# A selective scan (Mamba-style) with its stage rebuilt: differences on row tiles, sums in 64x64 quarters, rows of C by DMA

## The reference, cut to what matters

```python
delta = softplus(pp[..., :D]); Bm = pp[..., D:D+N]; Cm = pp[..., D+N:]
A = -exp(A_log);  dA = delta * A;  A_bar = exp(dA)
U = X_main * (A_bar - 1)/dA * delta * Bm
H_t = A_bar_t * H_(t-1) + U_t          # per sequence, d, n, over t
y_t = sum_n C_t[n] * H_t[:, n]
Y_proj = (y * silu(Xn @ W_up2.T)) @ W_down.T + b_down
out = X_res + Y_proj
```

## Time and profile before

| | us |
|---|---|
| median of 3 runs | 694.96 |
| span of the profiled execution | 668.4 |
| first scan to last (L509) | 106.3 to 373.6 |
| TensorE busy, of the span | 546.2 (82%) |
| VectorE busy | 510.2 (76%) |
| GpSimd busy | 432.6 (65%) |
| ScalarE busy | 338.0 (51%) |

### The profile page before, as it was taken

The page is one execution under the profiler, slowest core; times in us unless marked ns, Lnnn a source line. Parts: engine busy times, 40 slices in busy tenths (PEclk is TensorE's granted clock), DMA queues, the critical chain, the costliest instruction groups (busy, mean ns, idle before and its releaser), DMA issues.

```text
span 668.4 us, 12960 instructions
## 1 busy us (share of the span) xinstructions
PE 546.2 (82%) x3471; PEld 410.1 (61%) x3472; DVE 510.2 (76%) x1227; ACT 338.0 (51%) x809; POOL 432.6 (65%) x539
## 2 busy tenths in 40 slices
PE   3598996889899989989949889980667999999990
PEld 2433344656676757666728757770535779999990
DVE  7657677999999999998999862464686776666654
ACT  1655767836576756675723144420584554444430
POOL 3205592889999999999994677756027743455550
PEclk9999997879999999999998999995687989999996
DMA  7999000020000000000120155557931121222106
GB/s 244 171 280 288 19 6 0 1 64 1 1 1 0 0 0 0 0 0 0 48 79 17 35 162 164 166 170 220 384 116 50 50 65 41 60 56 59 50 24 188
DMA packets 55017, 54.83 MB, mean 82 GB/s; under 512 B 7743, under 2 KB 44182, under 8 KB 53952
## 3 DMA queue, kind: packets, MB, share of 16 engines
q1 hardware_dynamic: 49584, 42.57, 21.2%
q0 software_dynamic: 5392, 11.76, 6.8%
HBM read 34.24 MB, written 21.12 MB: 83 GB/s over the span
## 4 chain that ended last, share of the span: by engine, by line
PE 48%; DVE 25%; issue 8%; POOL 6%; ACT 6%; DMA 5%; DVEq 1%; SPq 0%; ACTq 0%; POOLq 0%
DVE arena L509 8%; PE bank L1419 7%; PE bank L1055 6%; PE bank L1406 6%; PE bank L1057 5%; PE bank L1014 4%; POOL expert_rows L1931 4%; POOL bd L1863 2%; PE bank L1098 2%; DVE arena L470 2%; PE bank L982 2%; PE bank L1023 2%; DMA xnw<-expert_rows 2%; DMA expert_rows<-gate,zbuf 1%; PE bank L1042 1%
## 5 line engine op out<-in xcount | busy, mean ns | idle before, releaser
L509 DVE TENSOR_TENSOR_SCAN arena<-bank,arena 128x256 f32<-128x256 f32 x256 | 160.9, 667 | 8.2 <-issue 6.1
L1553 ACT ACTIVATE arena<-delta,nega 128x256 f32<-128x256 f32 (+1 forms) x256 | 108.0, 499 | 8.8 <-DVE delta L428 6.9
L1879 POOL TENSOR_TENSOR arena<-arena 128x256 f32<-128x256 f32 x116 | 89.0, 771 | 24.7 <-DVE arena L470 20.2
L1055 PE MATMUL bank<-bd,xnw 128*128 128x258 f32 x256 | 86.4, 420 | 20.3 <-DVE arena L509 16.3
L1981 POOL DMA_INDIRECT pair_rows<-w1b,xnT x48 | 50.8, 1058 | 58.2 <-DVE w1b L771 49.3
L470 DVE SCALAR_TENSOR_TENSOR arena<-arena,inva,bank 128x256 f32<-128x256 f32 x192 | 82.6, 456 | 0.1
L1854 POOL TENSOR_TENSOR bd<-cfs,btok 128x258 f32<-128x258 f32 x128 | 79.3, 640 | 0.0
L1057 PE MATMUL bank<-bd,xnw 128*128 128x256 f32 x256 | 79.3, 392 | 0.0
L1055 PEld LDWEIGHTS bank<-bd,xnw 128*128 128x128 f32 x256 | 44.7, 196 | 44.9 <-DVE arena L509 24.5
L1014 PE MATMUL bank<-arena,ident 128*128 128x256 f32 x232 | 71.0, 388 | 1.3 <-DVEq L483 0.9
L1536 ACT ACTIVATE hbuf<-bank,inva 128x256 f32<-128x256 f32 x64 | 26.8, 469 | 83.2 <-PE bank L1042 83.0
(11 more groups left out here) (294 smaller groups left out, 1099.7 us busy)
## 6 DMA issues: line engine op xcount, KB each, us to landing
expert_rows<-bd SPq DMA_DIRECT2D x8, 1024.0 KB, 9.8
xnT<-expert_rows SPq DMA_DIRECT2D x4, 1024.0 KB, 6.2
bd<-in_w SPq DMA_DIRECT2D x4, 1024.0 KB, 13.2
arena<-in_w SPq DMA_DIRECT2D x4, 1024.0 KB, 14.4
slots_in<-bd POOLq DMA_DIRECT2D x1, 3120.0 KB, 24.7
xnT<-slots_in SPq DMA_DIRECT2D x48, 65.0 KB, 1.8
xnw<-expert_rows SPq DMA_DIRECT2D x3, 1024.0 KB, 6.4
bd<-in_w SPq DMA_DIRECT2D x8, 256.0 KB, 4.2
```

Source lines behind the costliest of these rows:

```text
L509: m = V.tensor_tensor_scan(zb[:, s % 8, r, :], dw_bank(par, s)[:, r * L:(r + 1) * L], abar[:, s % 8, r, :], 0.0, ALU.add, ALU.mult)
L1055: pe.matmul(o[:, :, 0:P + 1], xT[:, par, 0, h * P:(h + 1) * P], bd[:, par, 0, 2 * n2:2 * n2 + 2, :], start=True, stop=False, skip_group_ch ...
L1553: m = nc.scalar.activation(abar[:, s % 8, r, :], delta[:, h, bass.ds(b * L, L)], ACT.Exp, scale=negs[:, h, n:n + 1])
L1879: nc.gpsimd.tensor_tensor(zb[:, s % 8, 0, :], zb[:, s % 8, 0, :], zb[:, s % 8, 1, :], ALU.add).then_inc(S["q_ready"], 1)
```

## The change

Only the scan stage and its edges change.

- Steps: step s now holds half `s // 2 % 2` of the channels and states `first_n(s)`, `first_n(s) + 1`; four steps share four states. The results live in a ring of 16 steps (before: 8 for A_bar and 8 for results), and the scan writes over A_bar in place.
- Differences (`fill`): x and B are laid out in windows of 44 time steps that give 43 differences, three windows for each half of time. The two halves of time lie on partitions 0 to 43 and 64 to 107, so that the matmuls of a pair are on different row tiles. One fill makes 4 states of one half of the channels, that is two steps, into two banks; there are two such pairs of banks. The band matrices are compact: one GpSimd operation of 516 elements for 4 states (`band`), its pattern loaded once.
- C: `c_spread` writes the 16 rows of C to DRAM and reads them back spread over all partitions, in two DMAs of 1 MB for each batch, double buffered. The split of C, the selector products and the scaled rows are gone.
- Products: one operation of 512 elements for both states of a step, result times C, on GpSimd for 14 of the 16 steps and on VectorE for steps 7 and 15 (in batch 7 for six steps).
- Sums (`y_pair`, `y_quarters`): TensorE multiplies by diagonal 64x64 matrices of 1/A (`dg`, made once by GpSimd), each 128x128 product cut into four quarters; the correction enters as the first term with weights -1 (`y_begin`), from one product on VectorE (`correction`) that reads PSUM.
- `finish` is one product with the gate out of PSUM. The output projection takes y as weights and gives tokens on partitions, so its result is added to the residual at once (`residual`, 256 elements a batch); the bias is added once on GpSimd. The 16 transposes and four sums behind the last batch are gone.
- Order: TensorE's queue is written anew, with fills of the next batch at the end of this one. ScalarE copies x instead of GpSimd. `down` of batch b comes in batch b+1.

The core of the diff (loads, names, memory layout and the other engines' deletions are cut; blank lines are left out):

```diff
+WN, WIN, WK = 3, 43, 44
+STARTS = (0, 43, 85)
+GW = WN * WIN * 4
+XW = STARTS[2] + P + 64
+BY_DVE = (7, 15)
+BY_DVE_LAST = (2, 4, 7, 10, 12, 15)
...
+        ring = arena[:, :].rearrange("p (s r l) -> p s r l", s=16, r=2)
...
+        xT = xnf[:, 0:1536].rearrange("p (a q d) -> p a q d", a=2, q=WN)
+        yg = xnf[:, 1536:2048].rearrange("p (j l) -> p j l", j=2)
+        t1 = hb[:, 0:512].rearrange("p (h l) -> p h l", h=NH2)
+        bands = [xnTw[:, :], hb[:, 2032:2032 + 4 * GW]]
...
+        def half(s):
+            return s // 2 % 2
+        def first_n(s):
+            return s // 4 * 4 + s % 2 * 2
...
+        def dw_view(s):
+            o = 2 if half(s) == 0 else 0
+            return banks[:, o:o + 2, :].rearrange("p j c -> p (j c)").rearrange("p (t n) -> p n t", n=4)
+        def c_view(par, s):
+            return cbc[par][:, first_n(s) * L:first_n(s) * L + 2 * L].rearrange("p (r l) -> p r l", r=2)
...
+            def mult(b, par, s, last=False):
+                if s == min(own_steps(last)) or s == min(k for k in own_steps(last) if k > 7):
+                    dve.wait_ge(S[f"c_in{par}{s // 8}"], c_count(b, par))
+                dve.wait_ge(S["scanned"], b * 16 + s + 1)
+                V.tensor_tensor(ring[:, s, :, :], ring[:, s, :, :], c_view(par, s), ALU.mult).then_inc(S["z_dve"], 1)
+            def correction(b):
+                dve.wait_ge(S["m_ready"], b + 1)
+                V.tensor_tensor(t1[:, :, :], xm[:, :, bass.ds(b * L, L)], bank[7][:, :].rearrange("p (h l) -> p h l", h=NH2), ALU.mult
+                                ).then_inc(S["t1_ready"], 1)
+            def finish(b):
+                dve.wait_ge(S["y_done"], b * 8 + 16)
+                dve.wait_ge(S["dn_ready"], b + 1)
+                V.tensor_tensor(yg[:, :, :], banks[:, 4:6, 0:L], gate[:, :, bass.ds(b * L, L)], ALU.mult).then_inc(S["yg_ready"], 1)
+            def residual(b, o):
+                dve.wait_ge(S["dn_ready"], b + 2)
+                if not later(b, 1):
+                    dve.wait_ge(S["bias_in"], 1)
+                t = acc[:, bass.ds(b * 2, 2), :].rearrange("p t d -> p (t d)")
+                V.tensor_tensor(t, t, o[:, 0:L], ALU.add).then_inc(S["dn_evac"], 1)
...
-                    dve.wait_ge(S["dw_ready"], b * 16 + s + 1)
-                    dve.wait_ge(S["p_free"], b * 16 + s + 1)
+                    if s % 2 == 0:
+                        dve.wait_ge(S["dw_ready"], b * 8 + s // 2 + 1)
                     for r in range(2):
-                        m = V.tensor_tensor_scan(zb[:, s % 8, r, :], dw_bank(par, s)[:, r * L:(r + 1) * L], abar[:, s % 8, r, :],
+                        m = V.tensor_tensor_scan(ring[:, s, r, :], dw_view(s)[:, 2 * (s % 2) + r, :], ring[:, s, r, :],
                                                  0.0, ALU.add, ALU.mult)
-                    m.then_inc(S["ab_free"], 1)
-                    if s >= 1:
-                        mult(b, s - 1)
-                    elif later(b, 1):
-                        mult(b - 1, 15)
+                    m.then_inc(S["scanned"], 1)
+                    if s == 0 and later(b, 1):
+                        mult(b - 1, 1 - par, 15)
+                    if s - 1 in own_steps(last):
+                        mult(b, par, s - 1, last)
                     if not later(b, 1) and s < 12:
                         dve.wait_ge(S["dve_link"], link.n)
                         if s < 4:
                             add_log(2 + s)
                         elif s >= 8:
                             last_steps(s - 8)
-                        dve_at["steps"] = link.n
+                        dve_at["steps" if s > 3 else "logs"] = link.n
+                    if s == 2:
+                        correction(b)
                     if s == 4 and later(b, 1):
-                        finish(b - 1, 1 - par)
+                        finish(b - 1)
+                    if s == 13 and later(b, 1):
+                        residual(b - 1, bank[6])
...
+            def c_spread(b):
+                par = b % 2
+                sp.wait_ge(S["pro_xe"], b + 1)
+                if b > 1:
+                    for k in range(2):
+                        sp.wait_ge(S[f"c_in{par}{k}"], b // 2 * 16)
+                sp.dma_start(crows[par, :].rearrange("(n l) -> n l", n=N), ccur[:, :]).then_inc(S["c_out"], 16)
+                if b == 1:
+                    sp.wait_ge(S["dve_link"], dve_at["placed"])
+                sp.wait_ge(S["c_out"], b * 16 + 16)
+                for k in range(2):
+                    if b > 1:
+                        sp.wait_ge(S["z_pool"], by_pool(b - 2, 8 * k + 7))
+                        sp.wait_ge(S["z_dve"], by_dve(b - 2, 8 * k + 7))
+                    sp.dma_start(cbc[par][:, 2048 * k:2048 * (k + 1)], crows[par, 2048 * k:2048 * (k + 1)].partition_broadcast(P)
+                                 ).then_inc(S[f"c_in{par}{k}"], 16)
...
+            def pro1(b):
                 pe.wait_ge(S["xcur_ready"], b + 1)
+                if later(b, 1):
+                    pe.wait_ge(S["t1_ready"], b)
+                    pe.wait_ge(S["dn_evac"], b)
                 for w in range(2):
                     for h in range(NH2):
+                        m = pe.matmul(M1[2 * N * w:2 * N * w + N, L:2 * L], wll[:, h, DI + w * N:DI + (w + 1) * N],
+                                      xcur[:, h, 1:1 + L], start=(h == 0), stop=(h == NH2 - 1), skip_group_check=True)
+                for q in range(WN):
+                    for h in range(NH2):
+                        o = M0[:, q * DI + h * P:q * DI + (h + 1) * P] if q < 2 else M1[:, h * P:(h + 1) * P]
+                        for j in range(2):
+                            at = STARTS[q] + P * j
+                            m = pe.matmul(o[64 * j:64 * j + 64, :], xcur[:, h, at:at + 64], ident[:, :], start=True, stop=True,
+                                          skip_group_check=True)
                 m.then_inc(S["pro_x"], 1)
...
+            def fill(b, par, u):
+                g, h = u // 2, u % 2
+                if h == 0:
+                    pe.wait_ge(S["bd_ready"], b * 4 + g + 1)
+                if u > 1 or later(b, 1):
+                    pe.wait_ge(S["scanned"], b * 16 + (2 * u - 2))
+                for q in range(WN):
+                    for j in range(2):
+                        rows = slice(64 * j, 64 * j + WK)
+                        m = pe.matmul(bank[(2 if h == 0 else 0) + j][:, 4 * STARTS[q]:4 * (STARTS[q] + WIN)], xT[rows, par, q, h * P:(h + 1) * P],
+                                      bands[par][rows, g * GW + q * 4 * WIN:g * GW + (q + 1) * 4 * WIN], start=True, stop=True,
+                                      skip_group_check=True)
+                m.then_inc(S["dw_ready"], 1)
+            def y_quarters(weights, moving, start, stop):
                 for h in range(NH2):
+                    for j in range(2):
+                        rows = slice(64 * j, 64 * j + 64)
+                        m = pe.matmul(bank[4 + j][64 * h:64 * h + 64, 0:L], weights(h)[rows, :], moving(h)[rows, :],
+                                      start=start, stop=stop, skip_group_check=True)
+                return m
+            def y_begin(b):
+                pe.wait_ge(S["t1_ready"], b + 1)
+                if later(b, 1):
+                    pe.wait_ge(S["yg_ready"], b)
+                pe.sem_inc(S["pe_past"], 1)
+                y_quarters(lambda h: halves[:, 1, :], lambda h: t1[:, h, :], True, False)
+            def y_pair(b, g, m, last=False):
+                steps = (4 * g + m, 4 * g + 2 + m)
+                pe.wait_ge(S["z_pool"], by_pool(b, max(s for s in range(steps[1] + 1) if s not in own_steps(last)), last))
+                if any(s in own_steps(last) for s in steps):
+                    pe.wait_ge(S["z_dve"], by_dve(b, steps[1], last))
+                pe.sem_inc(S["pe_past"], 1)
                 for r in range(2):
+                    n = 4 * g + 2 * m + r
+                    done = y_quarters(lambda h: dg[n // 8][:, n % 8, h, :], lambda h: ring[:, steps[h], r, :],
+                                      False, g == 3 and m == 1 and r == 1)
+                done.then_inc(S["y_done"], 1)
...
+                last = not more
+                fill(b, par, 2)
+                if later(b, 1):
+                    for m in range(2):
+                        y_pair(b - 1, 3, m)
+                fill(b, par, 3)
+                if more:
+                    pro1(b + 1)
+                else:
+                    compact(0)
+                fill(b, par, 4)
+                y_begin(b)
+                for m in range(2):
+                    y_pair(b, 0, m, last)
+                if last:
+                    compact(1)
+                fill(b, par, 5)
+                if more:
+                    pro2(b + 1)
+                fill(b, par, 6)
+                if last:
+                    compact(2)
+                for m in range(2):
+                    y_pair(b, 1, m, last)
```

(28 more changed lines are left out.)

461 lines of the change are left out of this document (162 added, 299 removed).

## The result

The kernel after takes 649.15 us (median of 4 runs, 645.93 to 652.12), the kernel before 695.08 us beside it: ratio 0.9313, 95% interval [0.9258, 0.9367]. (The two medians alone give 0.934, inside that interval.) Forecast were 641.4 us and 628 to 667. A second set gave 647.92 us and 0.9316 [0.9265, 0.9368].

The account below looks back on a forecast made before the run. Three engines were taken to bound the scan stage together, VectorE setting the pace. Savings of 37.2 (steady), 6.8, 3.8, 1.5 and 4.3 us sum to 53.6: 668.4 - 53.6 + 26.6 = 641.4 us, range 628 to 667.

Parts of the forecast that it names:

- Steady batches: Scan stage, batches 1 to 6: 25.5 us a batch instead of 31.7, 10% over the fullest engine, saving 37.2 us.
- Own products: VectorE's two 512-wide multiplications a batch, both operands in SBUF: 0.87 us each, between 0.69 and 2 us.
- Batch 0: First batch of the scan stage: 31.5 us instead of 38.3, saving 6.8 us.
- A wait of over 1 us at step 8: Scan stage: VectorE waiting that long for fill 4 would show the forecast wrong.
- Batch 7: Last batch of the scan stage: 35 us to its last scan instead of 38.8, saving 3.8 us.
- Start: Before the first scan: first fill comes before the softplus is through, saving 1.5 us.
- End: From the last scan's end to GpSimd's gather: 6.9 to 7.2 us instead of 11.5, saving 4.3 us.
- Around the span: Whole run: the 26.6 us between profiled span 668.4 and median 695.0 were kept as a fixed difference.
- GpSimd as the bound: Rival, scan stage: products at 1.48 and bands at 1.28 us give a period of 28, 660 us; chance 0.18.
- Covers on TensorE: Rival, scan stage: two TensorE stretches outlast VectorE's work beside them, period 28.1, 661 us; chance 0.15.
- No tiles at once: Rival, TensorE in the scan stage: tiles do not run together, 52.7 us a batch, 851 us; chance 0.03.
- The clock: Rival: TensorE, less busy, could fall to 1.2 GHz; half clock throughout gives 757 us; chance 0.05.

Follow-up runs that it names:

- last_order: Kernel after with batch 7's second compaction moved ahead of the sums and VectorE's index readings at steps 8 and 12 instead of 6 and 11: 644.58 us, ratio 0.9253.
- second profile: The kernel before, unchanged, run and profiled once more: 695.65 us, ratio 1.0002, span 696.6 us.
- quick execution: The first profiled execution of the kernel before, unchanged, from which the prediction worked: span 668.4 us, where its timed runs were 694.96 us.

## Why the prediction held, and where it was off

**Steady batches: right in kind, 1.4 us a batch too slow.** VectorE was to take 22.6 us, and is busy 132.43/140 x 24.12 = 22.8, of which 1.1 us are waits inside its own products that the 22.6 did not have. GpSimd was to take 23.2 and has 14 x 1.31 + 4 x 1.05 + 0.63 = 23.2 by the single rows, 22.4 by its busy share. The terms for a wide product (1.27, measured 1.31), a band (1.05, measured 1.048) and a pair of scans (1.18 both) hold. The four-element inner run costs nothing that shows. TensorE was to take 22.6: a fill with its change of shape was put at 1.07 us and takes 1.08, 32 sums at 1.93 and take 1.89. Only the B and C projection was overpriced, at 1.7 us: its 8 instructions take 1.05, where one by one they would take 1.7; the two column tiles work at once. The stretch fill, projection, transposes, fill was put at 5.6 us and takes 4.6 (174.56 to 179.15). So the cover that I saw as just fitting has room, and a batch runs 4% over its fullest engine, not 10%. These 4% are a mean: under 1% in the quick batches, and in the others 1.7 us for VectorE's long product and 1.65 more where the clock fell. That is 6 x 1.4 = 8.4 us better than forecast.

**Own products: the mean was inside the bounds, the single wait was not.** 0.87 us was taken and 1.40 measured; the bound of 2 us was for one long GpSimd instruction each time, and single products took up to 2.78. With one operand in PSUM an instruction of the same size keeps to 0.67 (L511). The Trainium skill (SBUF — State Buffer, Who interferes with whom) says that whoever issues first has the shared pair for the whole instruction and the other is blocked. The trace agrees for the first of them, and goes further: VectorE's product, there since 191.75, also waited for the GpSimd product that began at 192.72. The price is not the wait alone: for VectorE's next scans GpSimd then stood 1.81 us and TensorE 2.48 us, and the clock fell.

**Batch 0: 34.2 us, forecast 31.5.** VectorE waits 2.46 us for fill 4 at 123.59, and the last softplus parts take 2.28 to 2.34 us a pair (1.61 to 2.10 before); GpSimd's longer instructions are the likely cause, not a shown one. A wait of over 1 us at step 8 was named as a sign of error. It appears here only, with the clock of the batch at 0.70; in two later batches it is 0.77 and 0.35 us.

**Batch 7: 42.2 us, forecast 35.** This is the step that failed. I summed VectorE's busy time to 34.3 us, which holds (33.4 measured, from 287.07 to 329.28), and added 0.7 for the order. VectorE waited 8.6 us in it for compactions that TensorE took behind sums at half clock (the third wait in the 9.0 above lies behind the last scan). With one compaction and two of VectorE's readings moved (last_order) the batch takes 35.4 us, with the clock still at 0.76; so it was the place in the queue.

**Start: forecast -1.5, measured +0.6** (+2.1 against the profile from which the forecast was made). The cost of GpSimd's bias sum moved into the search was put at nothing. It holds VectorE for 3 us, and taking it away brought the first scan 3.2 us forward.

**End: forecast -4.3, measured -1.6** by the last scan to the memset. From the end of the last scan at 329.3 the first gather behind the last wait for indices is reached 10.6 us later, at 339.87; forecast 7.2. VectorE's timeline:

```profile
329.28 2.40 DVE L499 TENSOR_TENSOR arena<-arena,bd 128x512 f32<-128x512 f32 x1
334.88 0.69 DVE L511 TENSOR_TENSOR xnw<-banks,gate 128x512 f32<-128x512 f32 x1 [3.20 <-PE banks L1102]
335.48 0.28 DVE L573 COPY banks<-cfs 128x128 f32<-128x128 f32 x1
```

The last product takes 2.40 us for the 0.9 counted, and two pairs of sums at the lower clock 3.3 us, where one pair at 1.2 was counted.

**The base.** "Around the span" there were 2 us, not 26.6. The sum to the median came out all the same, since the quick execution's gain lay behind the scan stage, where nothing was changed. The measured difference, by spans, is 46.5 us against 53.6: scan stage 48.5 against 47.8 (steady batches better by 8.4, batches 0 and 7 worse by 9.9; 2.0 came back because the stage of before is 2.0 us longer in its second profile, the rest is in how the stretches are cut), start and end 1.0 against 5.8, and 3.0 us of scatter in unchanged code. That the stage as a whole came out within 1 us of its forecast is luck: two errors of 8 to 10 us with opposite signs.

**Rivals.** GpSimd as the bound: right that it binds in the quick batches (22.32 of 22.45 us), wrong in its prices. Covers on TensorE: they hold. No tiles at once: out (its 851 us should have been 845 by its own terms). The clock: it did not fall throughout, but it was nearer than its 0.05 says. The rival counted an average, a cost from 23% of the time at half clock on. Batch 3 had 0.93, which is 14%, and lost 1.65 us, because the slow stretch lies just behind a wait, where there is nothing to spare. The cost is paid in batches 0 and 7 (clock 0.70 and 0.72) and in batches 1, 3 and 5 (0.92 to 0.93), and leaving out work in a steady batch was enough to lose 3.2 us in each. The clock at 1.0 in batches 1 to 6 was one of the forecast's own signs; it was 0.97.
